# A mixture-of-experts kernel on one core: an expert's fifth group in two halves of 128 rows, and a third group without a branch

## The chip, the cores and the metric

The kernel runs on 1 core of one Trainium2 chip. The metric is the device time of one execution in microseconds, lower is better; of the kernel before it is 2322.14 us, the median of 3 runs.

## What is computed

Two layers work on x, 4096 token rows (32 sequences of 128) of 512 numbers: a recurrent scan and an attention first, then a gated attention form (mLSTM), and last the mixture of experts, which the change is about. Cut to that last part:

```python
probs = softmax(x @ gate_w)                 # 4096 x 32 experts
w, sel = top_k(probs, 8); w = w / w.sum()
C = 2 * (T * 8 // E)                        # 2048 slots per expert
...
g = einsum('ech,ehi->eci', xg, w_gate)      # rows of the expert, 512 -> 192
u = einsum('ech,ehi->eci', xg, w_up)
y = einsum('eci,eih->ech', silu(g) * u, w_down)
out = zeros.at[t_slot].add(w_slot[:, None] * y)
```

Each token goes to 8 experts, so there are 32768 pairs and an expert gets 1024 rows on average. With the given inputs the router's counts are, for experts 0 to 31: 865, 1198, 1120, 963, 980, 1318, 1132, 826, 922, 771, 793, 1100, 1074, 906, 950, 764, 1375, 1158, 1055, 904, 1123, 973, 953, 1137, 1139, 1051, 1334, 698, 1116, 1033, 1077, 960.

## The kernel before

The first 1260 us are the other layers and the router; they are in a block of their own that the change leaves alone. The second block is the experts. An expert's rows are taken in groups of `GROUP` = 256, as many groups as its count needs: `NGRP` = 8 at most, `USUAL` = 5 of them written out and the rest in a loop. Each engine runs its own program over the experts, and they meet only at semaphores.

For one group GpSimd gathers 2 x 128 rows of 512 numbers by index into `xg` (L1753) and later scatters the weighted results with an add into the output (L1761), from one of three buffers of `y`. TensorE does, in this order (`turn`, `down`, `gate_up`):

- 8 transposes of the gathered rows into PSUM (L1858);
- the down products of the group before, 10 of 512 columns (L1867 to L1881), which wait for `hx2`, `hh1` and `hl1`;
- gate and up of this group. Weights and rows are split into a high and a low part in float16 (`wh`, `wl`, `xh`, `xl`), and each product is high x high, low x high and high x low over 4 pieces of the 512 inputs. There are three outputs of 128 rows: `gate` (PSUM bank 2), the second part of gate and up together (bank 3), `up` (bank 4). That is 3 x 12 = 36 products of 256 columns (L1887, L1888 with `xh`, L1892 with `xl`). The order is: 16 products with `xh`, then the wait for `xl`, 8 with `xl` that make bank 3 (`gate2_ps`) and bank 2 (`gate_ps`) ready, then 12 for `up`.

ScalarE copies half of the transposed rows to `xh` (L1980), scales the down results of the group before into `y` (L1964), notes the group's row numbers and weights (L1972, L1973), and applies silu to bank 3 (`s2`, L1987, after `gate2_ps`) and bank 2 (`s1`, L1990, after `gate_ps`). VectorE casts the other half of `xh` (L2047), makes `xl` in two pieces (L2051, L2055), and multiplies silu and up into the high and low parts of the gated rows (`gated`, L2038 to L2042), first the 64 rows of the second part (`hx2`), then the 128 (`hh1`, `hl1`). In an expert's first two groups ScalarE and VectorE also split the next expert's weights.

Each engine reads the expert's count into a register (`count_of`) and branches on it ahead of groups 2 to 7 (counted from 0). TensorE and VectorE use `written_out_groups`; ScalarE runs a loop of three turns over two groups each; GpSimd's program is written out for all 32 experts. The loop over experts takes two per turn (`pairs_of_experts`), the weights being double-buffered, and the last two experts are written out behind it: the loop's back edge comes behind every expert with an odd number.

Of the kernel before, what the change touches and what calls it, by code (L numbers as in the profile page):

```python
# [13 lines left out]
P = 128  # L14
# [6 lines left out]
def build(nc, x, ctx_in, w, u, Wa, Wp, w_std, w_rec, Wi, bi, Wf, bf, ln_scale, gate_w, w_gate, w_up,  # L21
# [6 lines left out]
    KC = D // P  # L28
# [20 lines left out]
    with ExitStack() as whole:  # L49
# [1609 lines left out]
        with ExitStack() as ctx:  # L1659
# [56 lines left out]
            def count_of(eng, e):  # L1716
                return eng.value_load(counts[0:1, bass.ds(e, 1)], min_val=1, max_val=CAP)

            def y_buffer(g):

                return YBUF - 1 if g == 0 else g % 2

            def written_out_groups(eng, n, group):

                for g in range(2, USUAL):
                    with eng.If(n > g * GROUP):
                        group(g, g)
                with eng.If(n > USUAL * GROUP):
                    group(USUAL, 2)
                    with eng.Fori(USUAL + 1, NGRP) as g:  # L1730
                        with eng.If(n > g * GROUP):
                            group(g, 3)
# [13 lines left out]
            def _(pool):  # L1746
# [18 lines left out]
                def add_rows(k):  # L1765
                    pool.reg_add(n_added[k], n_added[k], 16)
                    for h in range(2):
                        pool.wait_ge(wy_ready[h], 1)
                        pool.sem_inc(wy_ready[h], -1)  # L1769
                        scatter(k, h)  # L1770
# [13 lines left out]
                def gather_group(e, g, b):  # L1784
                    col = e * (CAP // P) + 2 * g
                    gather(b, lambda h: slot_t[:, col + h, 0:1])

                def expert(e):
                    n = pool.value_load(counts[0:1, e:e + 1], min_val=1, max_val=CAP)
                    with pool.If(n > 2 * GROUP):  # L1790
                        gather_group(e, 2, 2)
                    add_rows(y_buffer(0))
                    with pool.If(n > 3 * GROUP):
                        gather_group(e, 3, 3)
                    earlier_experts_added()
                    add_rows(y_buffer(1))
                    more = e + 1 < ne
                    if more:
                        with pool.If(n <= 4 * GROUP):
                            gather_group(e + 1, 0, 0)  # L1800
                    with pool.If(n > 2 * GROUP):
                        with pool.If(n > 4 * GROUP):
                            gather_group(e, 4, 4)
                        add_rows(y_buffer(2))
                    if more:
                        with pool.If(n <= 4 * GROUP):
                            gather_group(e + 1, 1, 1)
                        with pool.If(n > 4 * GROUP):
                            gather_group(e + 1, 0, 0)
                    with pool.If(n > 3 * GROUP):  # L1810
                        with pool.If(n > USUAL * GROUP):
                            gather_group(e, USUAL, 2)
                        add_rows(y_buffer(3))
                    with pool.If(n > 4 * GROUP):
                        if more:
                            gather_group(e + 1, 1, 1)
                        add_rows(y_buffer(4))
                    with pool.If(n > USUAL * GROUP):
                        add_rows(y_buffer(USUAL))
                    for g in range(USUAL + 1, NGRP):  # L1820
                        with pool.If(n > g * GROUP):
                            gather_group(e, g, 3)
                            add_rows(y_buffer(g))
# [21 lines left out]
            def _(pe):  # L1845
# [37 lines left out]
                def gate_up(j):  # L1883
# [22 lines left out]
                    with_xh(P, 4)  # L1906
                    with_xl(P, 4, up_ps)

                def expert(e, j, more):
                    turn(0)  # L1910
                    down(1 - j, 0)
                    pe.wait_ge(wh_ready[j], 1)
                    pe.sem_inc(wh_ready[j], -1)
                    gate_up(j)

                    def group(g, b):
                        turn(b)
                        down(j, b)
                        gate_up(j)
                    group(1, 1)  # L1920
                    n = count_of(pe, e)
                    written_out_groups(pe, n, group)

                pe.wait_ge(id_ready, 1)
# [9 lines left out]
            def _(act):  # L1934
# [57 lines left out]
                def expert(e, j, more):  # L1992
                    c0 = e * (CAP // P)
                    group(c0, y_buffer(0), (lambda: split_gate_up(1 - j)) if more else None)
                    group(c0 + 2, y_buffer(1), (lambda: split_down(1 - j)) if more else None)
                    n = count_of(act, e)
                    with act.Fori(1, NGRP // 2) as two:
                        for g in range(2):
                            with act.If(n > two * (2 * GROUP) + g * GROUP):
                                group(c0 + two * 4 + 2 * g, y_buffer(2 + g))  # L2000

                act.preload_act_table_set("silu_and_others")
                split_gate_up(0)
# [98 lines left out]
```

## Time and profile before

| | us |
|---|---|
| median of 3 runs | 2322.14 (2321.32 to 2324.43) |
| span of the profiled execution | 2363.2 |
| TensorE products, busy in it | 2153.1 (91%) |
| TensorE weight loads | 1618.5 (68%) |
| VectorE | 1603.3 (68%) |
| GpSimd | 1489.4 (63%) |
| ScalarE | 1134.5 (48%) |

The page gives the profiled execution's span, from its first instruction to its last, and no other time of that execution; it is 41 us above the median of the runs, which were not profiled. Times of single instructions come from that one execution. A product's duration runs from its issue to its modelled end, and products overlap in the array, so the pace is read from one start to the next. In a timeline "x8" means eight instructions merged into one row.

### The profile page before, as it was taken

How to read it: one execution, taken by the hardware profiler on the slowest of the kernel's cores; microseconds unless marked ns; L12 is line 12 of the kernel's file. 1: busy time of each engine (PE TensorE's matmuls, PEld its weight loads, DVE VectorE, ACT ScalarE, POOL GpSimd, SP SyncE). 2: the span in 40 equal slices, each digit the busy share in tenths (PEclk: the TensorE clock that was granted, in tenths of full speed). 3: DMA queues.
4: the chain of work that ended last, by engine and by line, in shares of the span. 5: the costliest groups of instructions: out<-in, count | busy, mean ns of one | idle time of the engine just before them, and what ended most of it. 6: DMA issues, size and time to landing. Idle time of an engine off the chain costs nothing. (4 is left out here: it accounts for less than half of the span.)

```text
span 2363.2 us, 61084 instructions
## 1 busy us (share of the span) xinstructions
PE 2153.1 (91%) x19896; PEld 1618.5 (68%) x19992; DVE 1603.3 (68%) x3221; ACT 1134.5 (48%) x2817; POOL 1489.4 (63%) x1673
## 2 busy tenths in 40 slices
PE   3899999999999999999834999999998999999997
PEld 2677777777767777777523676777776777777775
DVE  5577777777767777777423666666666676666664
ACT  1454554554554554555312544555454555554553
POOL 5226556656656656656456777777776777777775
PEclk9999999999999999999957999999999999999999
DMA  3010010010010010010103888677887788887776
GB/s 121 15 38 27 27 36 27 27 36 27 28 35 27 27 36 27 28 34 23 39 14 92 166 177 186 140 173 169 179 176 177 148 173 182 182 175 154 172 150 98
DMA packets 141437, 222.51 MB, mean 94 GB/s; under 512 B 32944, under 2 KB 65840, under 8 KB 141360
## 3 DMA queue, kind: packets, MB, share of 16 engines
q0 software_dynamic: 74752, 144.02, 31.2%
q1 hardware_dynamic: 62000, 69.24, 9.7%
q10 hardware_dynamic: 4608, 8.39, 0.9%
q8 instruction: 28, 0.46, 0.1%
q14 instruction: 49, 0.40, 0.1%
HBM read 136.34 MB, written 96.73 MB: 99 GB/s over the span
## 5 line engine op out<-in xcount | busy, mean ns | idle before, releaser
L1761 POOL DMA_INDIRECT out_dram<-y,m_add x300 | 501.7, 1672 | 203.6 <-POOLq L1769 143.7
L1887 PE MATMUL ps<-xh,wh 128*128 128x256 f16 x1752 | 399.7, 273 | 7.3 <-PEq L1899 4.7
L1888 PE MATMUL ps<-xh,wl 128*128 128x256 f16 x1752 | 399.5, 273 | 0.0
L1753 POOL DMA_INDIRECT xg<-z_scratch,slot_t x292 | 297.1, 1017 | 94.5 <-issue 86.8
L650 POOL DMA_INDIRECT slot_scratch<-pair,slots x248 | 251.4, 1014 | 99.9 <-issue 41.8
L1964 ACT ACTIVATE y<-ps,wts_now 128x512 f32<-128x512 f32 x294 | 185.5, 682 | 153.8 <-ACTq L1963 149.9
L1016 PEld LDWEIGHTS ps<-xnT,wqk 128*128 128x128 f32 x2048 | 238.7, 194 | 16.9 <-issue 16.9
L1016 PE MATMUL ps<-xnT,wqk 128*128 128x128 f32 x2048 | 241.6, 277 | 1.7 <-PEq L1263 1.7
L1892 PE MATMUL ps<-xl,wh 128*128 128x256 f16 x1752 | 239.0, 273 | 0.0
L2038 DVE SCALAR_TENSOR_TENSOR hx<-ps,s 64x256 f16<-64x256 f32 x146 | 62.2, 426 | 245.6 <-issue 168.6
L1887 PEld LDWEIGHTS ps<-xh,wh 128*128 128x128 f16 x1752 | 171.7, 98 | 53.4 <-issue 21.5
L1888 PEld LDWEIGHTS ps<-xh,wl 128*128 128x128 f16 x1752 | 171.7, 98 | 32.4 <-issue 0.6
L1858 PE MATMUL ps<-ident,xg 128*128 128x128 f32 x1168 | 152.8, 274 | 37.1 <-DMA xg<-z_scratch,slot_t 33.7
L1980 ACT ACTIVATE xh<-ps 128x512 f16<-128x512 f32 x146 | 87.2, 597 | 204.0 <-ACTq L1979 151.0
L1892 PEld LDWEIGHTS ps<-xl,wh 128*128 128x128 f16 x1752 | 171.4, 98 | 19.8
L1858 PEld LDWEIGHTS ps<-ident,xg 128*128 128x128 f32 x1168 | 132.4, 141 | 40.6 <-DMA xg<-z_scratch,slot_t 34.7
L1867 PE MATMUL ps<-dh,hx 128*128 128x512 f16 x294 | 112.2, 382 | 25.2 <-PEq L1864 15.8
L2039 DVE SCALAR_TENSOR_TENSOR h<-ps,s 64x256 f32<-64x256 f32 (+1 forms) x292 | 121.8, 417 | 0.0
L1029 PE MATMUL ps<-wa,xnT 128*128 128x512 f32 x256 | 118.4, 605 | 0.0
L2047 DVE CAST xh<-ps 128x512 f16<-128x512 f32 x146 | 100.1, 685 | 27.0 <-DVEq L2046 18.4
L1875 PE MATMUL ps<-dh,hh 128*128 128x512 f16 x294 | 112.7, 383 | 4.8 <-PEq L1872 3.1
L2055 DVE TENSOR_TENSOR xl<-ps,xh 128x512 f16<-128x512 f32 x146 | 100.9, 691 | 21.5
(279 smaller groups left out, 4659.0 us busy)
## 6 DMA issues: line engine op xcount, KB each, us to landing
wst<-in_L_ffn_w_gate_dram SPq DMA_DIRECT2D x32, 384.0 KB
wst<-in_L_ffn_w_up_dram SPq DMA_DIRECT2D x32, 384.0 KB
xt<-in_x_dram SPq DMA_DIRECT2D x32, 256.0 KB, 2.6
ct<-in_ctx_dram SPq DMA_DIRECT2D x32, 256.0 KB
out_dram<-x SPq DMA_DIRECT2D x32, 256.0 KB
z_scratch<-zn ACTq DMA_DIRECT2D x32, 256.0 KB
wdst<-in_L_ffn_w_down_dram SPq DMA_DIRECT2D x32, 256.0 KB
out_dram<-y,m_add POOLq DMA_INDIRECT x300
```

What stands on the lines that cost most here:

```text
L650: pool.indirect_dma_start(out=slot_d[:, :], out_offset=bass.IndirectOffsetOnAxis(ap=slots[:, k:k + 1], axis=0), in_=pair[:, k, :], in_offs ...
L1016: m = pe.matmul(ps[:, bank, c * T:(c + 1) * T], wqk[:, k, j, 4 * c:4 * c + 4, :].rearrange("p h d -> p (h d)"), xnT[:, k, :], start=(k == ...
L1029: m = pe.matmul(ps[:, V_BANK, :], xnT[:, k, :], wa[:, k, 2 * H * DS:2 * H * DS + D], start=(k == 0), stop=(k == KC - 1))
L1753: pool.indirect_dma_start(out=xg[b][:, h, :], out_offset=None, in_=z_d[:, :], in_offset=bass.IndirectOffsetOnAxis(ap=rows(h), axis=0)).the ...
L1761: pool.indirect_dma_start(out=acc_d[:, :], out_offset=bass.IndirectOffsetOnAxis(ap=m_add[:, k, h:h + 1], axis=0), in_=y[:, k, h, :], in_of ...
L1858: m = pe.transpose(ps[:, bank, c0:c0 + P], xg[b][:, h, k * P:(k + 1) * P], ident[:, :])
L1875: pe.matmul(o, hh1[:, t], dh[:, j, 0, :], start=False, stop=False)
L1887: pe.matmul(ps[:, dst, 0:GROUP], wh[:, j, k, c0:c0 + P], xh[:, k, :], start=(k == 0), stop=False)
L1888: pe.matmul(ps[:, dst, 0:GROUP], wl[:, j, k, c0:c0 + P], xh[:, k, :], start=False, stop=False)
L1892: m = pe.matmul(ps[:, dst, 0:GROUP], wh[:, j, k, c0:c0 + P], xl[:, k, :], start=False, stop=(k == KC - 1))
L1964: act.activation(y[:, k, h, :], ps[:, 5 + h, :], ACT.Copy, scale=wts_now[:, h:h + 1])\
L2039: dve.scalar_tensor_tensor(full, up, 1.0 / WSC, s, ALU.mult, ALU.mult).then_inc(dve_step, 1)
```

## The change

It does two things.

The fifth group (`b == USUAL - 1`, the group number 4) gets its own form of gate and up on TensorE, `gate_up_by_halves`. All waits, for both parts of `xh` and for `xl`, come first. Then, only if the count is over 4 x 256 + 128 = 1152, come the 36 products for the second 128 rows, and after them always the 36 for the first 128. Each product has 128 columns, and each output is finished before the next one begins. The signals `gate2_ps`, `gate_ps` and `up_ps` come from the first half's products, which are last. The other engines, the transposes and the down products still handle 256 rows. For this the count is loaded on TensorE ahead of group 1, no longer after it.

The third group (number 2) has no branch any more on any engine. On ScalarE it is written out ahead of the loop, the loop has two turns over the groups 3 and 4, then 5 and 6, and group 7 stands behind it with a branch of its own.

```diff
             def written_out_groups(eng, n, group):
-                for g in range(2, USUAL):
+                group(2, 2)
+                for g in range(3, USUAL):
                     with eng.If(n > g * GROUP):
                         group(g, g)
...
                 def expert(e):
                     n = pool.value_load(counts[0:1, e:e + 1], min_val=1, max_val=CAP)
-                    with pool.If(n > 2 * GROUP):
-                        gather_group(e, 2, 2)
+                    gather_group(e, 2, 2)
...
-                    with pool.If(n > 2 * GROUP):
-                        with pool.If(n > 4 * GROUP):
-                            gather_group(e, 4, 4)
-                        add_rows(y_buffer(2))
+                    with pool.If(n > 4 * GROUP):
+                        gather_group(e, 4, 4)
+                    add_rows(y_buffer(2))
...
+                def gate_up_by_halves(j, n, most):
+                    halves = (slice(P, GROUP), slice(0, P))
+                    def with_xh(c0, dst, t):
+                        for k in range(KC):
+                            pe.matmul(ps[:, dst, t], wh[:, j, k, c0:c0 + P], xh[:, k, t], start=(k == 0), stop=False)
+                            pe.matmul(ps[:, dst, t], wl[:, j, k, c0:c0 + P], xh[:, k, t], start=False, stop=False)
+                    def with_xl(c0, dst, t):
+                        for k in range(KC):
+                            m = pe.matmul(ps[:, dst, t], wh[:, j, k, c0:c0 + P], xl[:, k, t], start=False, stop=(k == KC - 1))
+                        return m
+                    pe.wait_ge(xh_low_k_pe, 1)
...
+                    pe.wait_ge(xl_ready, 1)
+                    pe.sem_inc(xl_ready, -1)
+                    with pe.If(n > most):
+                        for c0, dst in ((2 * P, 3), (0, 2), (P, 4)):
+                            with_xh(c0, dst, halves[0])
+                            with_xl(c0, dst, halves[0])
+                    with_xh(2 * P, 3, halves[1])
+                    with_xl(2 * P, 3, halves[1]).then_inc(gate2_ps, 1)
+                    with_xh(0, 2, halves[1])
+                    with_xl(0, 2, halves[1]).then_inc(gate_ps, 1)
+                    with_xh(P, 4, halves[1])
+                    with_xl(P, 4, halves[1]).then_inc(up_ps, 1)
...
                     gate_up(j)
+                    n = count_of(pe, e)
                     def group(g, b):
                         turn(b)
                         down(j, b)
-                        gate_up(j)
+                        if b == USUAL - 1:
+                            gate_up_by_halves(j, n, g * GROUP + P)
+                        else:
+                            gate_up(j)
                     group(1, 1)
-                    n = count_of(pe, e)
                     written_out_groups(pe, n, group)
...
                     n = count_of(act, e)
-                    with act.Fori(1, NGRP // 2) as two:
-                        for g in range(2):
+                    group(c0 + 4, y_buffer(2))
+                    with act.Fori(1, NGRP // 2 - 1) as two:
+                        for g in (1, 2):
                             with act.If(n > two * (2 * GROUP) + g * GROUP):
                                 group(c0 + two * 4 + 2 * g, y_buffer(2 + g))
+                    with act.If(n > (NGRP - 1) * GROUP):
+                        group(c0 + 2 * (NGRP - 1), y_buffer(NGRP - 1))
```

On TensorE, in the fifth group, from the last down product on, the order before is this (`ps` is PSUM; the first wait is for both parts of `xh`):

```order
L1881 MATMUL ps<-dh,hl1 128x512
L1887 MATMUL ps<-xh,wh 128x256 [waits xh_low_k_pe,xh_high_k_pe]
L1888 MATMUL ps<-xh,wl 128x256
...
L1892 MATMUL ps<-xl,wh 128x256 [waits xl_ready]
L1892 MATMUL ps<-xl,wh 128x256 x7
```

Between the first products with `xh` and the one that waits for `xl` stand 16 products. Of the change, in the same place:

```order
L1880 MATMUL ps<-dh,hl1 128x512
L1928 COMPARE_AND_BRANCH [waits xh_low_k_pe,xh_high_k_pe,xl_ready]
L1914 MATMUL ps<-xh,wh 128x128
L1915 MATMUL ps<-xh,wl 128x128
...
L1919 MATMUL ps<-xl,wh 128x128 x4
L1928 UNCONDITIONAL_BRANCH
L1914 MATMUL ps<-xh,wh 128x128
L1915 MATMUL ps<-xh,wl 128x128
```

All three waits now stand on the branch, ahead of every product, and `xl` is used from the ninth product on instead of the 17th.

On ScalarE, after the silus of the second group, the order before:

```order
L1990 ACTIVATE s1<-ps 128x256 [waits gate_ps]
L1717 ISA
L1717 TENSOR_LOAD counts
L1717 ISA x2
L1997 UNCONDITIONAL_BRANCH
L1997 ISA
L1999 COMPARE_AND_BRANCH
L1980 ACTIVATE xh<-ps 128x512 [waits rows_ps_act]
```

and of the change:

```order
L2023 ACTIVATE s1<-ps 128x256 [waits gate_ps]
L1717 ISA
L1717 TENSOR_LOAD counts
L1717 ISA x2
L2013 ACTIVATE xh<-ps 128x512 [waits rows_ps_act]
```

The load of the count stays where it was; the loop's entry and the branch have moved behind the third group.

## Rows read from the trace of the kernel before

**Rows 1.** Table of stretches, 1500 to 2280 us: busy time and instructions by engine.

```profile
core 0: us, PE busy (x) PEld busy (x) DVE busy (x) ACT busy (x) POOL busy (x), PEclk, DMA share, GB/s
...
1500.00:2280.00 780.00, 753.53 (x5785) 572.26 (x5783) 527.58 (x1056) 392.69 (x972) 577.12 (x429) 1.00 0.80 172
```

**Rows 2.** Who waited for whom, TensorE, 1500 to 2280: us, times, longest.

```profile
PE ps L1867 <- PEq L1864: 11.6, 18, 2.3
...
PE ps L1858 <- issue: 0.4, 1, 0.4
```

**Rows 3.** Timeline of TensorE, fifth group of expert 18: start us, us, instruction.

```profile
1904.14 1.04 PE L1858 MATMUL ps<-ident,xg 128*128 128x128 f32 x8
1905.01 0.38 PE L1867 MATMUL ps<-dh,hx 128*128 128x512 f16 x1
...
1907.17 0.27 PE L1887 MATMUL ps<-xh,wh 128*128 128x256 f16 x1
...
1908.91 1.04 PE L1892 MATMUL ps<-xl,wh 128*128 128x256 f16 x8
...
1911.10 1.04 PE L1858 MATMUL ps<-ident,xg 128*128 128x128 f32 x8
...
1914.13 0.27 PE L1887 MATMUL ps<-xh,wh 128*128 128x256 f16 x1
```

**Rows 4.** Timeline of VectorE, the same stretch.

```profile
1907.24 0.69 DVE L2055 TENSOR_TENSOR xl<-ps,xh 128x512 f16<-128x512 f32 x1
1910.16 0.43 DVE L2038 SCALAR_TENSOR_TENSOR hx<-ps,s 64x256 f16<-64x256 f32 x1 [2.23 <-issue]
...
1911.08 0.42 DVE L2042 TENSOR_TENSOR hx<-h,hx 64x256 f16<-64x256 f32 x1
...
1912.96 0.69 DVE L2047 CAST xh<-ps 128x512 f16<-128x512 f32 x1
```

**Rows 5.** Timeline of ScalarE, the same stretch.

```profile
1908.95 0.20 ACT L1973 ACTIVATE wts_now<-slot_t 128x2 f32 x1
1909.64 0.38 ACT L1987 ACTIVATE s<-ps 64x256 f32<-64x256 f32 x1 [0.48 <-ACTq L1986]
```

**Rows 6.** The page's costliest groups: VectorE's gating of bank 3, one per group.

```profile
L2038 DVE SCALAR_TENSOR_TENSOR hx<-ps,s 64x256 f16<-64x256 f32 x146 | 62.2, 426 | 245.6 <-issue 168.6
```

**Rows 7.** Timeline of VectorE, fifth group of expert 11 and first of 12.

```profile
1673.65 0.43 DVE L2038 SCALAR_TENSOR_TENSOR hx<-ps,s 64x256 f16<-64x256 f32 x1 [2.23 <-issue]
...
1676.91 0.69 DVE L2047 CAST xh<-ps 128x512 f16<-128x512 f32 x1 [0.57 <-DVEq L2046]
```

**Rows 8.** Timeline of TensorE, the first gate/up product behind that cast.

```profile
1677.75 0.27 PE L1887 MATMUL ps<-xh,wh 128*128 128x256 f16 x1
```

**Rows 9.** Branches in TensorE's queue: duration ns min/median/max (loop edge; branches between groups).

```profile
L1710 PEldq COMPARE_BRANCH  x15: 76/221/226, 1344.7 to 2279.7; - x15
...
L1726 PEldq COMPARE_BRANCH  x96: 65/73/240, 1287.4 to 2346.8; - x96
```

**Rows 10.** Who waited for whom, GpSimd, 1500 to 2280 us.

```profile
POOL out_dram L1761 <- POOLq L1769: 98.5, 88, 4.5
```

**Rows 11.** Instruction packets, 1255 to 1356 and 1356 to 2290; TensorE's timeline at 1345.

```profile
q8 instruction: 6, 0.10, 0.4%
...
q8 instruction: 1, 0.02, 0.0%
...
1345.27 0.43 PE L1858 MATMUL ps<-ident,xg 128*128 128x128 f32 x2 [1.63 <-issue]
```

**Rows 12.** Timeline of TensorE in the router: products of 32 columns, one weight load.

```profile
166.57 0.19 PE L1165 MATMUL ps<-selb,ustrict 128*128 128x32 bf16 x1
166.59 0.10 PEld L1166 LDWEIGHTS ps<-selacc,onesb 128*128 128x128 bf16 x1
166.61 0.18 PE L1166 MATMUL ps<-selacc,onesb 128*128 128x32 bf16 x1
```

**Rows 13.** Timeline of ScalarE, second group of expert 10.

```profile
1623.89 0.38 ACT L1987 ACTIVATE s<-ps 64x256 f32<-64x256 f32 x1 [1.71 <-ACTq L1986]
```

**Rows 14.** Timeline of TensorE, the down behind it.

```profile
1625.89 0.38 PE L1867 MATMUL ps<-dh,hx 128*128 128x512 f16 x1 [0.66 <-PEq L1864]
```

More of the change, by code:

```diff
@@ L1907, in gate_up @@
                     with_xl(P, 4, up_ps)
+                def gate_up_by_halves(j, n, most):
[9 more added lines that the diff above has]
+                    pe.wait_ge(xh_low_k_pe, 1)
+                    pe.sem_inc(xh_low_k_pe, -1)
+                    pe.wait_ge(xh_high_k_pe, 1)
+                    pe.sem_inc(xh_high_k_pe, -1)
+                    pe.wait_ge(xl_ready, 1)
[10 more added lines that the diff above has]
+                    with_xl(P, 4, halves[1]).then_inc(up_ps, 1)
                 def expert(e, j, more):
```

## The prediction

> **What bounds the kernel now.** First the table of stretches: in the undisturbed part of the expert loop TensorE is busy for 753.5 of 780 us, GpSimd for 577 and the others less [rows 1]. Then the list of who waited: of TensorE's 26 idle us there the largest part stands before the first down product, where it waits for the gated rows, and only one wait of 0.4 us stands before a group's transposes [rows 2]. So every product that TensorE is spared is worth its time, unless a wait takes its place, and the branches and the load of the count between two groups, which come ahead of those transposes, cost nothing now.
>
> The timeline of one fifth group (expert 18, 1055 rows) shows the period: transposes at 1904.14, down at 1905.01, gate/up at 1907.17, the next expert's transposes at 1911.10, 6.96 us in all [rows 3]. Ten down products of 512 columns take 2.16 us, 0.216 each; the 16 gate/up products of 256 columns from 1907.17 to 1908.91 take 0.109 each. The difference is 0.107 for 256 columns, so **128 columns should take 0.109 - 0.053 = 0.056 us**.
>
> The second thing to see is when the operands are there. In the same group VectorE ends `xl` at 1907.24 + 0.69 = 1907.93 [rows 4], 0.76 us after gate/up began. Now that is free, since the first 16 products don't need `xl`. ScalarE has noted rows and weights by 1908.95 + 0.20 = 1909.15, and starts the silu of gate's second part (`s2`) at 1909.64 [rows 5]; VectorE's gating begins 0.52 later and its cast for the next group 2.80 later still [rows 4].
>
> **How often.** The router's counts on the given inputs give 146 groups, as many as the profile has gatings [rows 6]. 17 experts have a fifth group. In 12 of them (2, 6, 11, 12, 18, 20, 23, 24, 25, 28, 29, 30) the count is at most 1152, so one half is enough; in 5 (1, 5, 16, 17, 26) both halves run. All 32 counts are over 512, so the third group always ran.
>
> **One half (12 times).** Removed: 36 products x 0.109 = 3.93 us; added 36 x 0.056 = 2.02. But all of `xl` must now be there before the first product, and the branch carries that wait, so it is taken with nothing queued on TensorE to cover it. The wake-up: a cast that ended at 1676.91 + 0.69 = 1677.60 [rows 7] was followed by gate/up at 1677.75 [rows 8], 0.15 us. A taken branch of TensorE's queue shows 0.22, one not taken 0.07 (medians of 221 ns at the loop's back edge and of 73 ns at L1726, mostly not taken) [rows 9]. So the half starts at 1907.93 + 0.15 + 0.22 = 1908.30, 1.13 late, and ends at 1910.32, 0.78 before 1911.10.
>
> Not all of it arrives. `gate2` is now ready with the 12th product, started at 1908.30 + 11 x 0.056 = 1908.92; before it was the 20th, at 1907.17 + 19 x 0.109 = 1909.24. So `s2`, and with it VectorE's chain, is only 0.32 sooner. TensorE's down then waits for `hx2`: 1911.08 + 0.42 - 0.32 + 0.15 = 1911.33 instead of 1910.32 + 0.87 = 1911.19; plus 2.16 is 1913.49, against 1914.13 [rows 3]: 0.64 gained. Where the next expert is an even one VectorE also passes the loop's back edge, its cast comes 3.26 us behind its gating (1673.65 to 1676.91 [rows 7]), and the next gate/up waits for that cast; there only the 0.32 is gained. Eight of the 12 go to an odd expert, four to an even one: 8 x 0.64 + 4 x 0.32 = **6.4 us gained**.
>
> **Both halves (5 times).** Start at 1907.93 + 0.15 + 0.07 = 1908.15, 72 x 0.056 = 4.03, end at 1912.18: 1.08 late. `gate2` comes with the 48th product, 1908.15 + 47 x 0.056 = 1910.78, 1.54 later than before, so the down waits for `hx2` until 1911.50 + 1.54 + 0.15 = 1913.19 and gate/up follows at 1915.35, 1.22 late. Experts 1 and 17 lead to an even expert, where the cast decides: 1.54 each. 3 x 1.22 + 2 x 1.54 = **6.7 us lost**.
>
> **The third group without a branch.** On TensorE the branch lies behind queued products [rows 2]. On VectorE and ScalarE it lies where both wait for the next transposes, and GpSimd waits 98 us of the 780 for `y` [rows 10], so its four branches fewer per expert shorten a wait. I take 0. If each exposed one were worth a taken branch, 31 x 0.22 = 6.8 us would be gained; that is the other end. Moving the load of the count on TensorE ahead of group 1: 0, by the same 0.4 us.
>
> **More code.** TensorE's program for an expert grows by 36 pairs of weight load and product on 7 x 54 = 378, a tenth. In the first pass of the loop six packets of 16 KB arrive on an instruction queue, and once TensorE stands 1.63 us with no releaser shown [rows 11]; I take that for one of them. A tenth of six, for the loop and again for the last two experts written out, is about one packet more; with one stall in six packets 0.3 us, ends 0 and 2 x 1.63 = 3.3.
>
> **Sum**: -6.4 + 6.7 + 0 + 0.3 = +0.6 us. The profiled execution's span is 2363.2, 41 us above the median of 2322.14, and no row says where that lies. All terms are differences of a few tenths, so I add them to the median: **2322.7 us**. A measurement of this kernel tells about 0.2% (4.6 us) from no change.
>
> **Rival 1, slower: weight loads set the pace of short products.** Every product has its own load of 128 columns, which shows about 0.10 us [rows 12]. At 256 columns it hides behind the product before. If a product could not start until its load had run its 0.10, half the columns would save almost nothing: one half ends 1908.30 + 3.60 = 1911.90, 0.80 late; both end 1908.15 + 7.20 = 1915.35, 4.25 late; 12 x 0.80 + 5 x 4.25 = 31 us, 2353. Against it: in the router a load began at 166.59 and its product at 166.61, 0.04 behind the product before it [rows 12]. It decides from a cadence of 0.067 on: a half then gains 0.39 (0.32 to an even expert), both lose 1.87, -4.4 + 9.4 = +5.0. The Trainium skill ("TensorE: Matmul & The Clock Gate", Back-to-back issue gap) gives some 81 ns for load and product pairs of 128 columns in a real kernel, and 56 ns isolated; by the 81 the same sum is 12 x 0.12 + 5 x 2.88 = 16 us, 2338, an estimate from that page. No row here has such pairs. Chance 0.13.
>
> **Rival 2, faster: the small waits go.** If VectorE's chain did not hold the down back, a half would give its whole 0.78 and both cost 1.08: 9.4 - 5.4 = 4.0 us gained, and with exposed branches of the third group up to 6.8 more. Also, about once an expert ScalarE's wait for `gate2` ends some 1.1 us late (silu at 1623.89 with 1.71 idle) and TensorE then waits 0.66 [rows 13, 14]; I don't know its cause, and ScalarE's code is laid out anew. Some 8 us in all, 2314. Against it: the rows put `s2` behind `gate2`, which I have counted. Chance 0.16.
>
> **Rival 3, slower: the loop's code is fetched again** or stalls at more places: the 3.3 us above and as much again, 2329. Six packets came in the first pass, and in the 934 us after it one [rows 11]. Chance 0.06.
>
> **The numbers.** Forecast 0.65, all of it within 0.2%; faster 0.16; slower 0.13 + 0.06 = 0.19. The range leaves out the farther half of rival 1 and the farther part of rival 2: 2314 to 2336.
>
> **What would show it.** In the new profile: gate/up products of 128x128 start 0.056 apart; before the first of them in a fifth group TensorE idles about 1 us, released by VectorE's `xl`; a group with one half is 6.2 us from transposes to transposes, one with both 8.0; after the former the down is held 0.1 by `hx2`. Third groups stay at 6.96. The forecast is wrong if the cadence is over 0.067, if the wait for `xl` is well over 1.1 us, if the four-group experts' times change too, or if instruction packets appear in the loop's later passes.

## The result and the profile after

| | us |
|---|---|
| kernel before, measured beside it (20 runs) | 2324.68 (2320.53 to 2330.35) |
| changed kernel (20 runs) | 2329.34 (2323.08 to 2337.95) |
| ratio, 95% interval | 1.0018 (1.001 to 1.0025): 4.2 us more (2.3 to 5.8) |
| span of its profiled execution | 2324.3 |
| TensorE products; weight loads, busy | 2135.4 (92%); 1602.2 (69%) |

The change costs a little: the loss is clear of the noise, at 0.18% it is just under the 0.2% that was set as the bound of no change, and its interval reaches over that bound. TensorE is busy for 17.7 us less than in the profile before (2153.1), or for 7.3 less than in a second profile of the kernel before (2142.7, e1 below), and the time did not follow.

The table of stretches of the new profile, in the undisturbed part (answers to rows 1, over 740 instead of 780 us):

```profile
core 0: us, PE busy (x) PEld busy (x) DVE busy (x) ACT busy (x) POOL busy (x), PEclk, DMA share, GB/s
1500.00:2240.00 740.00, 718.24 (x5782) 547.64 (x5781) 518.63 (x1038) 388.75 (x955) 567.91 (x421) 1.00 0.82 176
```

Who waited for whom on TensorE, 1400 to 2240 us (answers to rows 2):

```profile
PE ps L1914 <- PEq L1927: 14.5, 14, 1.1
PE ps L1886 <- PEq L1898: 5.9, 13, 1.0
PE ps L1857 <- DMA xg<-z_scratch,slot_t: 3.5, 2, 2.0
```

The new wait is the first row: 14 fifth groups in this stretch, each with about 1 us of idle time between the last down product and the first short one. TensorE's queue (PEq) stands there at `xl_ready`. It is the wait that the prediction put there.

Timeline of TensorE, the fifth group of expert 18 (one half; answers to rows 3):

```profile
1874.95 1.04 PE L1857 MATMUL ps<-ident,xg 128*128 128x128 f32 x8
...
1879.22 0.23 PE L1914 MATMUL ps<-xh,wh 128*128 128x128 f16 x1 [1.07 <-PEq L1927]
1879.29 0.22 PE L1915 MATMUL ps<-xh,wl 128*128 128x128 f16 x1
1879.34 0.22 PE L1914 MATMUL ps<-xh,wh 128*128 128x128 f16 x1
...
1881.02 0.39 PE L1919 MATMUL ps<-xl,wh 128*128 128x128 f16 x4
1881.24 1.04 PE L1857 MATMUL ps<-ident,xg 128*128 128x128 f32 x8
1882.31 0.38 PE L1866 MATMUL ps<-dh,hx 128*128 128x512 f16 x1
...
1884.47 0.27 PE L1886 MATMUL ps<-xh,wh 128*128 128x256 f16 x1
```

From 1879.22 to 1881.24 there are 36 products: 0.056 us each, though each has its own weight load. The group takes 1881.24 - 1874.95 = 6.29 us instead of 6.96.

The same of the fifth group of expert 17, where both halves run:

```profile
1838.41 1.04 PE L1857 MATMUL ps<-ident,xg 128*128 128x128 f32 x8
...
1842.51 0.22 PE L1914 MATMUL ps<-xh,wh 128*128 128x128 f16 x1 [0.91 <-PEq L1927]
...
1846.53 0.71 PE L1857 MATMUL ps<-ident,xg 128*128 128x128 f32 x5
```

Its first product comes 4.10 us into the group, and the group takes 8.12 us.

Timeline of ScalarE and then of VectorE in the same group (answers to rows 5 and 4):

```profile
1878.17 1.26 ACT L1997 ACTIVATE y<-ps,wts_now 128x512 f32<-128x512 f32 x2 [1.80 <-PE ps L1880]
1879.78 0.20 ACT L2005 ACTIVATE rows_now<-slot_t 128x2 uint32 x1 [0.35 <-ACTq L2000]
1879.89 0.20 ACT L2006 ACTIVATE wts_now<-slot_t 128x2 f32 x1
1880.30 0.38 ACT L2020 ACTIVATE s<-ps 64x256 f32<-64x256 f32 x1 [0.20 <-ACTq L2019]
```

```profile
1878.06 0.69 DVE L2091 TENSOR_TENSOR xl<-ps,xh 128x512 f16<-128x512 f32 x1
1880.82 0.43 DVE L2074 SCALAR_TENSOR_TENSOR hx<-ps,s 64x256 f16<-64x256 f32 x1 [2.07 <-DVEq L2097]
1881.73 0.43 DVE L2078 TENSOR_TENSOR hx<-h,hx 64x256 f16<-64x256 f32 x1
...
1883.64 0.69 DVE L2083 CAST xh<-ps 128x512 f16<-128x512 f32 x1
```

`xl` ends at 1878.06 + 0.69 = 1878.75 and the first product comes at 1879.22, 0.47 later. The silu `s2` starts at 1880.30, 5.35 into the group, against 5.50 before (1909.64 - 1904.14 [rows 3, 5]). Right ahead of it ScalarE has scaled `y` and made its two notes, which end at 1880.09.

Beyond single groups I compare the mean distance from a group's transposes to the next group's, over experts 2 to 29, with the same kernel before in a profile of its own (the first experiment):

| group | before, again | changed |
|---|---|---|
| groups 1 and 3 | 6.96 | 6.96 |
| third group (2); the median is 6.96 in both | 7.10 | 7.10 |
| fifth, one half | 6.96 | 6.29 |
| first group behind it, odd expert (7 in the stretch) | 6.96 | 7.15 |
| first group behind it, even expert in the loop (3) | 7.08 | 7.50 |
| first group behind it, expert 30 (1) | 6.96 | 7.25 |
| fifth, both halves (4) | 6.96 | 8.12 to 8.16 |
| what follows it | 7.08 even (1); 7.05 sixth group (3) | 7.54; 7.10 |

One half thus saves 0.67 us and gives back 0.19 (odd) or 0.42 (even): net 0.48 and 0.25. Both halves cost about 1.23, or 1.62 where an even expert follows. Two of the 17 fifth groups can't be read this way, those of experts 1 and 30: in both kernels they lie where code is run for the first time, and take 10.16 and 9.58 us before, 9.40 and 10.95 changed.

### The profile page after: what moved, and what is told of

The parts are those of the page before. It is cut to its first block and busy times, and to the rows that moved or that the text cites. A ratio compares the mean times of both kernels' runs of the same rounds, so it can differ in the third digit from the quotient of the medians.

```text
span 2324.3 us, 61263 instructions
## 1 busy us (share of the span) xinstructions
PE 2135.4 (92%) x20171; PEld 1602.2 (69%) x20172; DVE 1602.9 (69%) x3221; ACT 1136.6 (49%) x2817; POOL 1484.7 (64%) x1673
## 3 DMA queue, kind: packets, MB, share of 16 engines
q10 hardware_dynamic: 4608, 8.39, 0.9%
## 5 line engine op out<-in xcount | busy, mean ns | idle before, releaser
L1886 PE MATMUL ps<-xh,wh 128*128 128x256 f16 x1548 | 351.9, 273 | 6.0 <-PEq L1898 5.9
L1887 PE MATMUL ps<-xh,wl 128*128 128x256 f16 x1548 | 351.9, 273 | 0.0
L1891 PE MATMUL ps<-xl,wh 128*128 128x256 f16 x1548 | 211.2, 273 | 0.0
L1886 PEld LDWEIGHTS ps<-xh,wh 128*128 128x128 f16 x1548 | 151.3, 98 | 45.2 <-issue 17.1
L1887 PEld LDWEIGHTS ps<-xh,wl 128*128 128x128 f16 x1548 | 151.4, 98 | 28.1
L1891 PEld LDWEIGHTS ps<-xl,wh 128*128 128x128 f16 x1548 | 151.4, 98 | 17.5
L1084 PE MATMUL ps<-wp,oT 128*128 128x512 f32 x256 | 115.2, 593 | 0.0
```

The costliest lines, as they stand in the source:

```text
L1084: m = pe.matmul(ps[:, PR_BANK, :], oT[:, k, :], wp[:, k, :], start=(k == 0), stop=(k == KC - 1))
L1886: pe.matmul(ps[:, dst, 0:GROUP], wh[:, j, k, c0:c0 + P], xh[:, k, :], start=(k == 0), stop=False)
L1887: pe.matmul(ps[:, dst, 0:GROUP], wl[:, j, k, c0:c0 + P], xh[:, k, :], start=False, stop=False)
L1891: m = pe.matmul(ps[:, dst, 0:GROUP], wh[:, j, k, c0:c0 + P], xl[:, k, :], start=False, stop=(k == KC - 1))
```

## The experiments

Three sets, each on a chip of its own and each beside runs of the kernel before: e1 to e4 (before: 2324.52 us, 33 runs), e5 to e8 (2325.26, 29 runs), e9 to e12 (2365.84, 24 runs). That third chip runs the kernel before 41 us slower; ratios are therefore always to the runs of the same set.

Where I speak of stretches, these are times of one profiled execution: "experts 0 and 1" is from the first transposes to those of expert 2, "2 to 29" the next one, "30 and 31" from there to the last group's start.

### e1: the kernel before again, with a profile

> The kernel before, unchanged, profiled and timed once more. Theory A (the late silus and the 41 us by which the first profile's span lay above the runs belong to that one execution): the ratio is 1.000 within 0.1%, the new span is 2320 to 2328 us, the groups of expert 10 are all 6.96 or 7.46 us, and TensorE's waits before the first down product (L1867) fall from 15.8 + 9.2 us to under 8. Theory B (they belong to ScalarE's code as it was laid out, and the change moved them away): span near 2360 again, one late silu per expert.

2325.13 us, ratio 0.9999 (0.999 to 1.0008); span 2325.0, not 2363.2. ScalarE's waits between 1350 and 2200 us in this profile:

```profile
ACT xh L1980 <- ACTq L1979: 178.4, 120, 3.5
ACT y L1964 <- ACTq L1963: 110.7, 79, 1.7
ACT s L1987 <- ACTq L1986: 61.8, 121, 1.6
```

In the first profile `s2` started over 6.2 us into the group in 43 of the 82 groups 1 to 3 of experts 2 to 29 (regular: 5.50), here in none of 82. The late silus of rows 13 were thus no part of the time that the medians measure on these chips, and nothing that a change could win there. So theory A held. All comparisons of profiles from here on to e8 are with this one, although e5 to e8 ran on another chip.

### e2 and e3: each half of the change alone

e2 is the kernel before with `gate_up_by_halves` and the earlier load of the count; e3 is the kernel before with the third group's branches gone:

```diff
-                for g in range(2, USUAL):
+                group(2, 2)
+                for g in range(3, USUAL):
```

> Only the fifth group's two halves (with the count loaded ahead of group 1); the third group keeps its branch. Theory A (the halves alone make the loss: fifth groups cost -0.48 us x 8, -0.26 x 4, +1.23 x 3, +1.62 x 2 = +2 us, and the longer program some 3 us more at code that is fetched for the first time): +3 to +6 us against before, ratio 1.001 to 1.0025, like the whole change. Rival (the branch of the third group, ScalarE's new layout above all, makes part of the loss): 0 to +2 us.

> Only the third group without its branch, on all engines; fifth groups as before. Theory A (the branch was hidden everywhere): within 0.05% of before, third groups 6.96 us as before. Rival, faster: each was exposed, up to 6.8 us less, ratio 0.997. Rival, slower: ScalarE's program is longer by one group and stands still more often where code is fetched for the first time, +1 to +3 us.

e2: 2329.52 us, ratio 1.0019 (1.0009 to 1.0029). e3: 2326.73, ratio 1.0004 (0.9995 to 1.0014). The loss is that of the halves, as theory A of e2 had it. The branch of the third group is worth nothing that can be measured, and the third groups keep their length; the 1 to 3 us more of e3's slower rival lie inside the interval.

### e4: both forms in the program, one of them run

The branch comes ahead of the waits, and the products keep the old order, 16 with `xh` ahead of the wait for `xl`:

```diff
-                            gate_up_by_halves(j, n, g * GROUP + P)
+                            with pe.If(n > g * GROUP + P):
+                                gate_up(j)
+                            with pe.If(n <= g * GROUP + P):
+                                gate_up(j, P)
```

> The change with one part made otherwise: the fifth group branches ahead of its waits, and runs either the old gate/up with 256 columns (count over 1152) or the old order with 128 columns (else). So the exposed wait for xl, the exposed branch and the second set of products are gone, the program stays as long. Theory A (those three are what the halves lose): one-half groups end about 1.9 us sooner, of which VectorE's chain lets 0.4 to 0.7 through, since ScalarE's silu cannot start before 1909.25 on the scale of rows 5: 8 x 0.7 + 4 x 0.4 = 7 us gained, groups with both halves 6.96 us again, and with 3 us for the code a ratio of 0.998 to 0.999. Rival (the program's length is the whole loss): ratio 1.000 to 1.001.

2330.40 us, ratio 1.0022 (1.0012 to 1.0032), over what either theory expected and as slow as the change, though the wait for `xl` is gone: no idle time ahead of the first short product, and groups with both halves are back at 6.96. TensorE, and then ScalarE, in the fifth group of expert 18:

```profile
1872.75 1.04 PE L1857 MATMUL ps<-ident,xg 128*128 128x128 f32 x8
...
1875.78 0.22 PE L1886 MATMUL ps<-xh,wh 128*128 128x128 f16 x1
1875.83 0.22 PE L1887 MATMUL ps<-xh,wl 128*128 128x128 f16 x1
...
1877.79 1.04 PE L1857 MATMUL ps<-ident,xg 128*128 128x128 f32 x8
1880.10 0.38 PE L1866 MATMUL ps<-dh,hx 128*128 128x512 f16 x1 [1.26 <-PEq L1863]
```

```profile
1875.96 1.26 ACT L1969 ACTIVATE y<-ps,wts_now 128x512 f32<-128x512 f32 x2 [1.80 <-PE ps L1880]
...
1877.69 0.20 ACT L1978 ACTIVATE wts_now<-slot_t 128x2 f32 x1
1878.09 0.38 ACT L1992 ACTIVATE s<-ps 64x256 f32<-64x256 f32 x1 [0.20 <-ACTq L1991]
```

The half group now takes 5.05 us, 1.24 less than in the change. But `s2` starts at 1878.09 - 1872.75 = 5.34, as in the change (5.35), again 0.2 behind the notes, and the down products wait 1.26. The group behind it is longer by as much (8.39), so the net gain of a half is 0.48 (odd) and 0.26 (even), as in the change. **What a half gives is set by ScalarE's order of work, not by when its products are ready.**

Over experts 2 to 29 the either form is ahead, 898.3 us against 902.7 (change), 902.0 (e3) and 904.1 (e1, with one group in it that is 1.7 longer than in e3). It loses that at experts 30 and 31: 70.1 against 61.2. The first group of expert 30 takes 14.21 us, where 6.96 was regular before and 8.4 is behind a half. TensorE there:

```profile
2241.18 0.49 PE L1891 MATMUL ps<-xl,wh 128*128 128x256 f16 x3
2245.59 1.23 PE L1891 MATMUL ps<-xl,wh 128*128 128x256 f16 x5 [3.91 <-issue]
```

TensorE stands for 3.91 us in the middle of eight like products, with no releaser. That is no semaphore. Expert 30 is the first behind the loop, and its code is run here for the first time. In e2 there is such a gap in the same group, which takes 11.53:

```profile
2252.20 0.58 PE L1892 MATMUL ps<-xl,wh 128*128 128x256 f16 x2 [2.78 <-issue]
```

The change itself has no such gap: its group there takes 7.25.

### e5 and e8: the longer program without the short products

The kernel before with 36 products per expert that are never entered, in e5 for every expert (shown), in e8 for the last two only (the outer condition there has `and isinstance(e, int)` too). The count is loaded ahead of group 1, as in the change:

```diff
+                        if b == USUAL - 1:
+                            with pe.If(n > CAP - 8):
+                                for r in range(9):
+                                    for k in range(KC):
+                                        pe.matmul(ps[:, 7, 0:P], wh[:, j, k, 0:P], xh[:, k, 0:P], start=(k == 0), stop=(k == KC - 1))
```

> The kernel before, plus, in each expert's fifth group ahead of its transposes, a branch that is never entered (count over 2040) around 36 products of 128 columns; the count is loaded ahead of group 1 as in the change. The branch is taken while TensorE has products queued. Theory A (what the change loses beyond its fifth groups, some 3.7 us, is the longer program where it is fetched for the first time): +2 to +5 us, ratio 1.001 to 1.002, with the middle experts' groups exactly as before and the loss in experts 0, 1, 30 and 31. Rival (it is something that the halves do there): ratio 1.000 within 0.0005.

> The same never-entered 36 products as in the first run of this call, but only in the two experts that are written out at the end. Theory A: +1 to +4 us, most of what the first run loses; the rest of it, 0 to 1.5 us, is the first pass of the loop. Rival: nothing.

e5: 2326.66 us, ratio 1.0005 (0.9996 to 1.0014). e8, with the fewer instructions: 2333.34, ratio 1.003 (1.0018 to 1.0042), 7.0 us more (4.2 to 9.8), above what theory A expected. So length as such does not cost. Nor does it matter by itself that the added code lies behind the loop, for e5 has it there too. Both have 29 instruction packets on TensorE's queue instead of 28. In e8 the time from the start of the last group to the end of the span is 28.3 us instead of 21.3. There, TensorE's last down products and the VectorE instruction that they need (`hx2`):

```profile
2314.73 0.59 PE L1867 MATMUL ps<-dh,hx 128*128 128x512 f16 x1 [5.77 <-PEq L1864]
```

```profile
2308.78 0.42 DVE L2047 TENSOR_TENSOR hx<-h,hx 64x256 f16<-64x256 f32 x1
```

`hx2` is complete at 2309.20, and TensorE starts 5.5 us later. The row names its queue, which elsewhere means a wait for a semaphore; here the operand had long been there. The source views show what the queue did: two branches, those of the groups that are not needed (`written_out_groups`; expert 31 has four groups, so the dead products lie inside the fifth group that it skips). L1726, then L1728 (duration ns min/median/max, start us):

```profile
L1726 PEldq COMPARE_BRANCH  x1: 2838/2838/2838, 2306.9 to 2306.9; - x1
L1728 PEldq COMPARE_BRANCH  x1: 4809/4809/4809, 2309.8 to 2309.8; - x1
```

The second ends at 2309.8 + 4.8 = 2314.6, and the product comes at 2314.73. In e1 the same L1728, first in the loop's later passes and then behind the last group:

```profile
L1728 PEldq COMPARE_BRANCH  x27: 68/222/235, 1373.1 to 2205.8; - x27
L1728 PEldq COMPARE_BRANCH  x1: 1979/1979/1979, 2309.1 to 2309.1; - x1
```

So a branch that shows at most 0.235 us in the loop's later passes takes 2.0 us (e1) and 4.8 us (e8) behind the last group, where this copy of it is passed for the first time. This is where e8 loses its 7 us. Not every first time is slow: in e1 the four copies of L1728 take 0.36, 4.46, 4.38 and 1.98 us.

### e6 and e7: the short forms in the loop only

e6 is e4, and e7 the change, with the plain `gate_up` in the two experts that are written out behind the loop (`and not isinstance(e, int)`).

> The version with either form of gate/up, but only inside the loop; the last two experts, which are written out, keep the plain form. Theory A: experts 2 to 29 as in the run before it (898 us where the kernel before takes 902 to 904), and the last experts back to about 61 us from 70, so -2 to -5 us against before, ratio 0.998 to 0.999. Rival (the loss at the end is not the written-out code): still 1.001 or more.

> The change, but the last two experts keep the plain form. Theory A: the fifth groups in the loop cost about +0.5 to +1 us in all, the first pass of the longer loop 1 us, the end nothing: ratio 1.0003 to 1.001. Rival (the halves themselves lose more than their groups show): 1.0018 as the change.

e6: 2330.53 us, ratio 1.0014 (1.0002 to 1.0025); e7: 2328.63, ratio 1.0013 (1.0004 to 1.0023). e6 doesn't get its loss back, as its rival expected; e7 lies between its two theories and decides nothing. In e6 the first group of expert 30 still takes 13.52 us, of which 3.5 with TensorE idle and no releaser, although its code there is that of the kernel before. So it is not the short form's own code at the end that is late; the stall sits behind the step out of the loop. e7, like the change, has none there (8.09 us for the group).

### e9 to e12: no code of TensorE behind the loop

TensorE's program doesn't use `more`, so its loop can run over all 16 pairs (the other engines keep their end):

```diff
-                pairs_of_experts(pe, expert)
+                with nc.Fori(0, ne // 2, engines=[pe.engine], hint_back_edge=True) as i:
+                    for j in range(2):
+                        expert(2 * i + j, j, True)
```

e9 is that on the kernel before, e10 on the change, e11 on e4. e12 is e11 with ScalarE's notes behind its silus:

```diff
                     weigh(k)
-                    note(col)
...
                     act.activation(s1[:, :], ps[:, 2, 0:GROUP], ACT.Silu, scale=1.0 / WSC).then_inc(s_ready, 1)
+                    note(col)
```

> The kernel before, with TensorE's loop over all 16 pairs of experts: the last pair is no longer written out behind the loop on TensorE (the other engines keep theirs). Theory A (what the halves and the either form lost is code run for the first time at the end, and of it mostly TensorE's): here little is lost to begin with, since in the profiles of the kernel before and of its repeat the first group of expert 30 took 6.96 us; only the fifth group of expert 30 (about 10.7) and the first of 31 (8.0) can shrink, by some 2 us if TensorE's code is what they wait for, and the time is 0 to 3 us under the kernel before. Theory B (those groups wait for the other engines' written-out code): nothing changes, within 1 us.

> The whole change, with TensorE's loop over all 16 pairs of experts. Theory A: what the change lost lies in TensorE's written-out end, so the ratio falls from 1.0018 to that of the kernel before with the same loop, within 0.5 us of it; in the profile every group of experts 30 and 31 has the length of its kind in the loop (6.96, 7.2 behind a half group, 6.96 otherwise), but for waits on other engines. Theory B (the loss is spread, or lies at the first experts): the ratio stays at 1.0015 to 1.002.

> The either form (36 products of 128 columns in the old order where the count ends in the first half, else the old 36 of 256), with TensorE's loop over all 16 pairs. The either form took experts 2 to 29 in 898.3 us against 902.0 to 904.1, and lost 8.9 us at experts 30 and 31 (70.1 against 61.2), of which 7.25 in one group, the first of expert 30. Theory A: the loss goes and the gain stays, so the time is 3 to 6 us under the kernel before (ratio 0.997 to 0.999). Theory B (the wait at the first group of expert 30 belongs to the other engines, which keep their written-out code): it stays, and the time is 3 to 6 us over.

> The same kernel, and ScalarE makes its notes of a group (two copies of 128 x 2, 0.4 us) behind both silus, no longer ahead of the first. In the half groups of the either form the first silu began 0.2 us behind the notes, 5.35 into the group, as late as in the halves of the change although its products were ready some 1.2 us sooner. Theory C (ScalarE's queue of work sets the half groups' net length): the silu begins about 4.95 into the half group, the next down product waits some 0.4 less (2.30 to about 1.9), and each of the 12 half groups saves 0.4 us more, 4 to 5 us in all against the same kernel with early notes. Rival D (VectorE's products behind the silu, or its xl, set it): the silu moves and the down products do not, within 1 us in all.

| | us | ratio (95%) | profile: 2 to 29 | 30 and 31 |
|---|---|---|---|---|
| e9 before, all in loop | 2363.77 | 0.9993 (0.9983 to 1.0003) | 938.7 | 62.0 |
| e10 change, all in loop | 2372.74 | 1.003 (1.0017 to 1.0043) | 940.9 | 63.4 |
| e11 either form, all in loop | 2366.47 | 1.0001 (0.999 to 1.0012) | 930.3 | 64.8 |
| e12 and late notes | 2357.32 | 0.9967 (0.9955 to 0.998) | 928.2 | 59.8 |

The packets of TensorE's code, in the profile of e1 and of e9 (whole span):

```profile
q8 instruction: 28, 0.46, 0.1%
```

```profile
q8 instruction: 21, 0.34, 0.1%
```

The seven that e1 has behind 1350 us are gone, so they were TensorE's written-out end.

**e9**: 2.1 us less or nothing; both theories allow it. The branch L1728 now takes 0.22 us there too:

```profile
L1728 PEldq COMPARE_BRANCH  x4: 222/225/234, 2244.4 to 2349.5; - x4
```

The fifth group of expert 30 shrinks from 9.58 (e1) to 6.96, as theory A had it, but the first of expert 31 grows from 8.57 to 12.01.

**e11** shows that the 14.21 us at expert 30 were TensorE's own code: its first group now takes 8.40, as behind any half, and experts 2 to 29 are 8.3 us under e9. Yet theory A's 3 to 6 us less did not come: the ratio is 1.0001. The first group of expert 31 takes 13.03 us (e9: 12.01, e1: 8.57), and VectorE, whose last two experts are still written out, stands there:

```profile
2316.78 0.69 DVE L2057 CAST xh<-ps 128x512 f16<-128x512 f32 x1 [3.53 <-issue]
```

This cast comes 1.9 us into a regular first group, 3.8 in e1, 5.6 in e9 and 6.6 here. So VectorE is late there in every one of them; most of what is more than in e1 comes with the loop over all pairs and not with the short products. The rest I can't place: the profiled execution of e11 took 2360.49 us, the shortest of its 12 runs and 6 under their median.

**e10** contradicts theory A for the change. It is 9.0 us over e9, where at most 0.5 was expected. With TensorE's end gone, the change still loses 7.1 us (4.0 to 10.2) against the kernel before, no less than with it. The profiles are 5.7 us apart, 2.1 of it ahead of the experts and 2.2 in experts 2 to 29.

**e12** confirms theory C. ScalarE and TensorE, the fifth group of expert 18:

```profile
1900.54 1.26 ACT L1971 ACTIVATE y<-ps,wts_now 128x512 f32<-128x512 f32 x2 [1.80 <-ACTq L1970]
1902.07 0.38 ACT L1993 ACTIVATE s<-ps 64x256 f32<-64x256 f32 x1 [0.27 <-ACTq L1992]
1902.35 0.37 ACT L1996 ACTIVATE s<-ps 128x256 f32<-128x256 f32 x1
1902.61 0.19 ACT L1979 ACTIVATE rows_now<-slot_t 128x2 uint32 x1
```

```profile
1897.33 1.04 PE L1857 MATMUL ps<-ident,xg 128*128 128x128 f32 x8
...
1902.37 1.04 PE L1857 MATMUL ps<-ident,xg 128*128 128x128 f32 x8
1904.07 0.38 PE L1866 MATMUL ps<-dh,hx 128*128 128x512 f16 x1 [0.65 <-PEq L1863]
```

`s2` starts 4.74 into the group instead of 5.35, and the down products wait 0.65 instead of 1.26. Where nothing else waits, a half and the group behind it need 12.83 us instead of 13.44, 0.61 less. With the waits that this chip adds in single groups the mean is 0.48 less than e11 where an odd expert follows (7 times in experts 2 to 29) and 0.35 less for an even one (4 times): 4.8 us, as expected. Rival D, by which the down products would stay, is out. The medians differ by 9.1 us. In the profiles experts 30 and 31 bring 5.0, and in 2 to 29 the 4.8 are partly taken back by single waits elsewhere (2.1 remain). e12 is **7.8 us faster than the kernel before** of its set (4.7 to 10.6), the only version here that is faster clear of the noise. Its notes come late in all 146 groups and not only in the halves, and late notes alone, on the kernel before, weren't tried; so how much of the 7.8 the halves bring is not shown. On the two chips of the first sets it wasn't run.

On this third chip `s2` of groups 1 to 3 starts over 6.2 us into the group in 42 of 81 (e9), 50 of 82 (e10), 40 of 82 (e11), 34 of 82 (e12), as in the profile ahead of the prediction.

## Why the prediction was right, and where it was not

The forecast was +0.6 us against the median of before, inside the bound of no change; measured are +4.2 (2.3 to 5.8). The case was right, but barely: the upper end of the interval is over the bound of 4.6. The size was 3.6 too small. 2329.34 lies inside 2314 to 2336; 2.5 us of its distance to 2322.7 are the kernel before, which measured 2324.68 beside it and not 2322.14.

- **128 columns take 0.056 us.** Right: 36 products in 2.02 us. Rival 1 is out with both its numbers. The Trainium skill ("TensorE: Matmul & The Clock Gate", Back-to-back issue gap) gives some 81 ns for pairs of weight load and product in a real kernel and 56 isolated; here a stream of such pairs keeps 56.
- **Start 1.13 late (one half), 0.98 (both).** 1.24 and 1.07 were measured (gate/up 4.27 and 4.10 into the group instead of 3.03). Wake-up and taken branch together are 0.47 behind `xl`, not 0.37.
- **Group of one half 6.2, both 8.0.** 6.29 and 8.12 to 8.16.
- **A half's net gain 0.64 (odd), 0.32 (even).** 0.48 and 0.25. This is the step that failed: "So `s2`, and with it VectorE's chain, is only 0.32 sooner." It was 0.15 sooner. I took the 0.40 us between the product that makes `gate2` and the silu as a fixed lag. But in rows 5 the notes end only 0.49 ahead of the silu. In the changed kernel they end 0.21 ahead of it, and 0.20 in e4, whose products are ready earlier. The later start alone, with the fixed lag, would have made the silu some 0.2 sooner (4.89 + 0.40 = 5.29 into the group); the notes take the rest, and by e4 an earlier start would have won nothing. The price by measured lengths is 8 x 0.48 + 4 x 0.25 = 4.8 us gained, not 6.4 (for expert 30's half 0.48 is assumed).
- **Both halves lose 1.22, or 1.54 to an even expert.** 1.23 and 1.62: 3 x 1.23 + 2 x 1.62 = 6.9, predicted 6.7; the 1.62 was measured at expert 17 and is assumed for expert 1.
- **Third group 0.** Right (e3). The other end, 6.8 us gained, is excluded. The reading of rows 2 behind it was incomplete: the 0.4 us was not the only wait ahead of a group's transposes. The same list has two more, of up to 2.0 us, for the gathered rows. They end with a transfer and not with a branch, so the 0 stands.

```profile
PE ps L1858 <- DMA xg<-z_scratch,slot_t: 3.8, 2, 2.0
```

- **Sum of the steady part**: 6.9 - 4.8 = +2.1, where the prediction had +0.3. That would be half of the measured loss. e4, which has no loss with both halves, bears it out: its experts 2 to 29 are 4.4 us under the change's. The stretch itself is too coarse for it: the same sum over experts 2 to 29 gives about +0.5, and the changed kernel takes 902.7 us there where versions with the old fifth group take 902.0 (e3), 902.7 (e8), 904.1 (e1) and 905.9 (e5).
- **More code 0.3, ends 0 and 3.3.** One packet more was right (29 instead of 28, none in the loop's later passes). The price was not: this is the other term that was mis-sized. What is left of the 4.2 is 2.1 (0.2 to 3.7). In the profiles the changed kernel has 1.0 more than e1 in experts 0 and 1, 0.7 in 30 and 31, and 1.6 behind the last group's start (but 2.7 less ahead of the experts and 1.3 less in 2 to 29, so that the spans differ by 0.7 the other way). For the 1.6 the traces name the place. It is the branch over the groups not needed, which takes 3.43 us there, against 1.98 in e1:

```profile
L1729 PEldq COMPARE_BRANCH  x1: 3427/3427/3427, 2306.8 to 2306.8; - x1
```

I had costed the packets by their number, with one stall of 1.63 us. The trace ahead of the prediction already had the branch that stands before it, L1728 behind expert 1, at 3.06 us, and the last one at 1.87:

```profile
L1728 PEldq COMPARE_BRANCH  x1: 3058/3058/3058, 1341.5 to 1341.5; - x1
L1728 PEldq COMPARE_BRANCH  x1: 1872/1872/1872, 2347.1 to 2347.1; - x1
```

e8 (+7.0), e5 (+1.2, not told from nothing) and e4's 3.91 us in one gap show that one packet's worth can cost anything from nothing to 7 us.
- **Rival 1's** sum at a cadence of 0.067 had a slip: `gate2` would then be only 0.20 sooner, so a half before an even expert gains 0.20 and not 0.32, and the sum is some +5.5. Nothing hangs on it, as the cadence is 0.056.
- **Rival 2** is out: VectorE's chain did hold the down back (0.67 of a half became 0.48), the third group's branches were worth nothing (e3), and of the late silus of rows 13 and 14 e1 has none.

**Open.** Where the code stalls is in part read from the traces: mostly on the branches that skip the groups not needed, when they are passed for the first time. Behind the last group this branch takes 1.98 us in e1, 2.98 in e5, 3.43 in the change and 4.81 in e8 (with 2.84 in the one ahead of it), and the time from the last group's start to the end is 21.3, 22.5, 22.9 and 28.3 us in this order. What decides how long each one takes is not settled. Length alone is out (e5 against e8), the short form's own code at the end too (e6), and TensorE's end alone as well (e10). The Trainium skill ("Runtime: NRT & Kernel Launch", Instruction fetch mechanics) says that code comes in blocks of 16 KiB, that crossing into the next one is mostly hidden, and that a taken branch to code not at hand must wait for the fetch. The traces agree with the branch: 1.98 to 4.81 us behind the last group against 0.22 in the loop's later passes, where no packet comes. "Mostly hidden" doesn't cover the gaps of 2.8 to 3.9 us in the middle of like products just behind the loop's end (e2, e4, e6). A trial that only shifts the code behind the loop by a few instructions wasn't made. Nor is it settled why e10 loses 9 us to e9, and what makes the third chip slower.

## What to carry to other kernels

Before you credit a shortened stage with its whole saving, list for every engine in its loop what it does between its input and its output: the net gain ends at the first one that has other work ahead of the urgent one, here two notes of 0.4 us ahead of a silu. Moving such work behind the urgent operation brought 9.1 us (e12 against e11, one chip), where cutting half of the products alone brought nothing that could be told (e11 against the kernel before). Treat code that is run only once, ahead of or behind a loop that is hot, as something with a price of its own, and look at the durations of its branches in the queue, not only at the engine's idle time. Keeping it in the loop took TensorE's own stalls at the end away, but brought no time that could be told from nothing (e9).

## What was not expected of the hardware

- A stream of 128-column products, each with its own weight load, keeps 0.056 us apart, about half of the 0.109 at 256 columns.
- Thirty-six products that are never run cost 7.0 us (4.2 to 9.8) when they lie only in the two experts behind the loop, and 1.2 (-0.9 to 3.3) when they lie in every expert, those two included.
- The branch over the groups not needed takes 0.07 to 0.235 us in the loop's later passes, and up to 5.1 us (e8, expert 1) where a copy of it is passed for the first time.
- The same program takes 2324.5 and 2325.3 us on two chips and 2365.8 on a third. There ScalarE's silu comes late in half of the groups 1 to 3, with the clock as before (0.977). The profile ahead of the prediction shows the same picture, and the three runs shown beside it don't.
